# A fused attention and sparse feed forward kernel on one core: the feed forward's x and inner values are turned by VectorE and device memory instead of TensorE

## The reference

```python
def ffn(x, c1_w, c2_w, w1, w2t):            # x: [2048, 512]
    inter = x @ c1_w.T @ c2_w.T             # rank 16, then 1792 wide
    blk = inter.reshape(2048, 56, 32)
    idx = argmax(blk, axis=-1) + arange(0, 1792, 32)   # one of each 32
    h = relu(einsum('bkm,bm->bk', w1[idx], x))
    return einsum('bk,bkm->bm', h, w2t[idx])

x = x + tanh(g_xattn[0]) * xattn(layernorm(x), ctx, mask, bias, Wq, Wk, Wv, Wo)
x = x + tanh(g_ffn[0]) * ffn(layernorm(x), c1_w, c2_w, w1, w2t)
```

## Time and profile before

| | |
|---|---|
| median of 3 runs | 1841.38 us (1840.96 to 1842.55) |
| the profiled execution | 1842.1 us |
| its span, first to last instruction | 1840.3 us |
| TensorE busy | 1818.5 us, 13916 matmul records |
| VectorE, ScalarE, GpSimd busy | 1148.5, 683.3, 844.5 us |
| moved by DMA | 359.34 MB |
| projections, attention, feed forward | to about 930, to about 1475, to the end |

### The profile page before, as it was taken

One profiled execution on the slowest core, in us unless ns is written; L12 is line 12 of the kernel. 1 busy time (PEld: TensorE's weight loads), 2 busy tenths in 40 slices (PEclk: granted clock), 3 DMA queues, 4 the chain that ended last, 5 costly groups with the idle time before them and its releaser, 6 DMA issues.

```text
span 1840.3 us, 35211 instructions
## 1 busy us (share of the span) xinstructions
PE 1818.5 (99%) x13916; PEld 1509.9 (82%) x13916; DVE 1148.5 (62%) x1798; ACT 683.3 (37%) x1761; POOL 844.5 (46%) x734
## 2 busy tenths in 40 slices
PE   9999999999999999999999999999999999999999
PEld 7788878788888878888878888888888888888887
DVE  6566567544556673334357666786667887777773
ACT  5232324322333343233345555555555422222221
POOL 7734538755334887778734343343433121111110
PEclk9999999999999999999999999999999999999999
DMA  5554556444444644467658878798787650000000
GB/s 223 189 176 179 200 195 240 149 180 176 177 164 153 204 165 167 163 227 247 212 232 350 325 289 328 285 388 327 296 326 274 250 206 24 24 24 24 24 12 18
DMA packets 114900, 359.34 MB, mean 195 GB/s; under 512 B 12080, under 2 KB 20656, under 8 KB 104240
## 3 DMA queue, kind: packets, MB, share of 16 engines
q1 hardware_dynamic: 114736, 357.09, 52.7%
HBM read 229.11 MB, written 127.93 MB: 194 GB/s over the span
## 4 chain that ended last, share of the span: by engine, by line
PE 60%; DVE 2%; DMA 0%; ACT 0%; issue 0%; DVEq 0%; ACTq 0%
PE bank L1535 17%; PE bank L1537 16%; PE bank L1536 16%; PE bank L1640 4%; PE bank L1604 3%; PE bank L1620 2%; PE bank L1753 1%; PE bank L1730 1%; DMA x_tile<-in_x 0%; PE bank L1709 0%; ACT scores L940 0%; DVE attn_sum L1343 0%; DVE scores L1229 0%; DVE attn_t_lo L1315 0%; DVE scores L1217 0%
## 5 line engine op out<-in xcount | busy, mean ns | idle before, releaser
L1535 PE MATMUL bank<-tokens_hi,wkq_hi 128*128 128x512 f32 x888 | 346.7, 390 | 6.5 <-issue 4.0
L1536 PE MATMUL bank<-tokens_lo,wkq_hi 128*128 128x512 f32 x888 | 345.6, 389 | 0.0
L1537 PE MATMUL bank<-tokens_hi,wkq_lo 128*128 128x512 f32 x888 | 345.5, 389 | 0.0
L802 POOL TENSOR_TENSOR wkq_lo<-raw_wkq,wkq_hi 128x768 fp32r<-128x768 f32 x126 | 276.6, 2215 | 129.7 <-ACT wkq_hi L904 129.7
L1535 PE MATMUL bank<-wo_hi,attn_t_hi 128*128 128x512 f32 x512 | 205.7, 402 | 1.2 <-DVE attn_t_lo L1315 1.2
L1535 PEld LDWEIGHTS bank<-tokens_hi,wkq_hi 128*128 128x128 f32 x888 | 166.7, 188 | 44.7 <-issue 5.9
L1537 PE MATMUL bank<-wo_hi,attn_t_lo 128*128 128x512 f32 x512 | 199.8, 390 | 0.0
L1536 PE MATMUL bank<-wo_lo,attn_t_hi 128*128 128x512 f32 x512 | 199.3, 389 | 0.0
L1537 PEld LDWEIGHTS bank<-tokens_hi,wkq_lo 128*128 128x128 f32 x888 | 166.7, 188 | 34.7
L1536 PEld LDWEIGHTS bank<-tokens_lo,wkq_hi 128*128 128x128 f32 x888 | 166.7, 188 | 34.3
L940 ACT ACTIVATE scores<-scores,negmax 128x64 f32<-128x64 f32 x512 | 172.2, 337 | 41.8 <-DVE negmax L1222 41.8
(11 more groups left out here) (140 smaller groups left out, 3705.8 us busy)
## 6 DMA issues: line engine op xcount, KB each, us to landing
k_t<-c SPq DMA_DIRECT2D x128, 256.0 KB, 2.0
v_by_token<-c SPq DMA_DIRECT2D x128, 256.0 KB, 2.0
q_t<-c SPq DMA_DIRECT2D x128, 256.0 KB, 2.3
kt<-k_t SPq DMA_DIRECT2D x16, 2048.0 KB, 9.2
qt<-q_t SPq DMA_DIRECT2D x16, 2048.0 KB, 13.7
v<-v_by_token SPq DMA_DIRECT2D x16, 2048.0 KB, 12.6
raw_wkq<-in_wk SPq DMA_DIRECT2D x32, 512.0 KB, 4.3
raw_wv<-in_wv SPq DMA_DIRECT2D x16, 1024.0 KB, 8.3
```

The costliest lines, as they stand in the source:

```text
L802: pool.tensor_tensor(lo, job_raw(r)[:, a:b, :].rearrange("p a (c w) -> p a c w", c=2), hi.bitcast(F32), ALU.subtract)\
L1535: pe.matmul(o, a[0], b[0], start=first_mm, stop=False, skip_group_check=not grouped)
L1536: pe.matmul(o, a[0], b[1], start=False, stop=False, skip_group_check=not grouped)
L1537: return pe.matmul(o, a[1], b[0], start=False, stop=last_mm, skip_group_check=not grouped)
```

## The change

The transposes leave TensorE. The norm of an x tile is written to one buffer (`fxn`), VectorE turns it in 32 x 32 blocks (one instruction, into `fxb`), SyncE stores it to device memory (`xf_d`) and loads it back with an address pattern that puts the blocks in their places (`xfr`). ScalarE makes the high part from there, and GpSimd, no longer VectorE, the low part (`pool_fx` counts them). The inner values go the same way, in two halves of 1024 and 768 (`turn_h`, `store_h`, `load_h`, `HALF`), and GpSimd makes their low parts (`pool_hl`). Rows of c1, w1 and w2 are reordered on the host to suit. c1 is stacked so that one matmul with the high part of x and one with the low part do the low rank product: 8 in place of 12.

Hidden products now run two tiles ahead of the output, selectors three, and VectorE, ScalarE and GpSimd follow. x is prepared one tile in each iteration, in place of two in every second; six tiles (`X_EARLY`) are normed and turned during the attention. Nine x buffers replace five. Three of the seven loads of w2 are issued from ScalarE's queue. The lines of the core, cut:

```diff
-X2R = 5
+X2R = 9
+X_EARLY = 6
+HALF = [(0, 1024), (1024, 768)]
...
+    sel, hid = (2, 3), (4, 5, 1, 6, 0)
...
+            def store_h(t, i):
+                sp.wait_ge(dve_hb, 2 * t + i + 1)
+                sp.dma_start(h_d[i][t], hmb[i][:, :]).then_inc(h_out[i], 16)
+
+            def load_h(t, i):
+                sp.wait_ge(h_out[i], 16 * (t + 1))
+                if t:
+                    sp.wait_ge(pool_hl, 4 * (t - 1) + 2 * i + 2)
+                sp.dma_start(hraw[i][:, :, :], h_d[i][t].rearrange("(q g) (r f) -> (g r) q f", q=4, r=4))\
+                    .then_inc(h_in[i], 16)
...
+            def fx_lo(t):
+                pool.wait_ge(act_fx, t + 1)
+                pool.tensor_tensor(xft_part(t, 1), by_chunk(xfr[t % 2], 0, CH), xft_part(t, 0).bitcast(F32), ALU.subtract)\
+                    .then_inc(pool_fx, 1)
+
+            def ht_lo(t, g):
+                pool.wait_ge(act_h, 4 * t + g + 1)
+                pool.tensor_tensor(hmt_part(g, 1), hraw_part(g), hmt_part(g, 0).bitcast(F32), ALU.subtract)\
+                    .then_inc(pool_hl, 1)
...
-            for j in range(PAIRS):
-                if j % 2 and j + 4 < PAIRS:
-                    do_rstd(LN + j + 3)
-                    do_rstd(LN + j + 4)
-                if j + 2 < PAIRS:
-                    rank(j + 2)
+            for g in range(4):
+                ht_lo(0, g)
+            for j in range(-1, PAIRS):
+                if j > 0:
+                    for g in range(4):
+                        ht_lo(j, g)
+                if j + 7 < PAIRS:
+                    do_rstd(LN + j + 7)
+                if j + 3 < PAIRS:
+                    rank(j + 3)
+                if j + 5 < PAIRS:
+                    fx_lo(j + 5)
...
+            load_w2(5)
+            load_w2(6)
+            load_w2(4)
+            for j in range(-1, PAIRS):
+                if j >= 0:
+                    for g in range(4):
+                        ht_hi(j, g)
                 for k in range(4):
...
+                    if j + 3 < PAIRS:
+                        sel(j + 3, k)
+                if j + 5 < PAIRS:
+                    fx_hi(j + 5)
...
+            def turn_h(t, i):
+                a, w = HALF[i]
+                dve.wait_ge(dve_hm, 4 * t + 2 * i + 2)
+                if t:
+                    dve.wait_ge(h_out[i], 16 * t)
...
+                dve.transpose(hmb[i][:, :], hm[:, a:a + w]).then_inc(dve_hb, 1)
...
+            for j in range(-1, PAIRS + 1):
+                if j < 0:
                     low_rank(1)
...
+                if 0 <= j and j + 6 < PAIRS:
+                    f_norm((j + 6,))
+                if j + 2 < PAIRS:
+                    block_rank(j + 2)
+                if j % 2 and 0 < j and j + 3 < PAIRS:
+                    low_rank((j + 3) // 2)
+                if j + 2 < PAIRS:
+                    first_max(j + 2)
+                if j > 0:
                     finish(j - 1)
                 for k in range(4):
...
+                        pick_h(j + 2, k)
+                        if k % 2:
+                            turn_h(j + 2, k // 2)
+                    if j + 3 < PAIRS:
+                        block_max(j + 3, k)
+                    if k == 2 and j + 7 < PAIRS:
+                        f_stats((j + 7,))
+                if j + 3 < PAIRS:
+                    mark_max(j + 3)
...
             def low_rank(u):
                 pe.wait_ge(*bank_free(("t", u)))
-                pe.wait_ge(dve_fx, 2 * u + 2)
+                pe.wait_ge(pool_fx, 2 * u + 2)
...
+            for j in range(1, PAIRS + 1):
                 for k in range(4):
                     output(j - 1, k)
-                    transpose_h(j, k)
...
+                    if j == 1 and k < 2:
+                        selector(3, k + 2)
+                    if k == 1 and j % 2 and j + 3 < PAIRS:
+                        low_rank((j + 3) // 2)
                 for k in range(4):
+                    if j + 2 < PAIRS:
+                        hidden(j + 2, k)
+                    if j + 3 < PAIRS:
+                        selector(j + 3, k)
```

More of the change, by code:

```diff
@@ new lines, in next_of @@
+    def next_of(banks, use):
+        k = used.get(banks, 0)
+        used[banks] = k + 1
+        return (use, banks[k % len(banks)])
+    sel, hid = (2, 3), (4, 5, 1, 6, 0)
+    out = [(("t", 0), 0), (("sel", 0, 0), 7), (("sel", 0, 1), 0)]
+    out += [next_of(sel, ("sel", 0, k)) for k in (2, 3)]
+    out += [next_of(sel, ("sel", 1, k)) for k in (0, 1)]
+    out += [next_of(hid, ("h", 0, k)) for k in (0, 1)]
+    out += [next_of(sel, ("sel", 1, k)) for k in (2, 3)]
+    out += [next_of(hid, ("h", 0, k)) for k in (2, 3)]
@@ new lines, in ffn_uses @@
+    out.append(next_of(sel, ("t", 1)))
+    out += [next_of(hid, ("h", 1, 0)), (("h", 1, 1), 7), next_of(sel, ("sel", 2, 0))]
+    for k in (2, 3):
+        out += [next_of(hid, ("h", 1, k)), next_of(sel, ("sel", 2, k - 1))]
+    out += [next_of(hid, ("h", 2, 0)), next_of(sel, ("sel", 2, 3))]
+    out.append(next_of(hid, ("h", 2, 1)))
+    for k in (2, 3):
+        out += [next_of(hid, ("h", 2, k)), next_of(sel, ("sel", 3, k - 2))]
+    for j in range(1, PAIRS + 1):
+        out.append(next_of(hid, ("out", j - 1)) if j == PAIRS - 1 else (("out", j - 1), 7))
+        if j == 1:
+            out += [next_of(sel, ("sel", 3, k)) for k in (2, 3)]
+        if j % 2 and j + 3 < PAIRS:
+            out.append(next_of(sel, ("t", (j + 3) // 2)))
+        for k in range(4):
@@ L160, in ffn_uses @@
             if j + 2 < PAIRS:
-                out.append((("sel", j + 2, k), 2 + k % 2))
-    out.append((("out", PAIRS - 1), 7))
-    return [(use, (0, 7, 2, 3, 4, 5, 6, 1)[b]) for use, b in out]
+                out.append(next_of(hid, ("h", j + 2, k)))
+            if j + 3 < PAIRS:
+                out.append(next_of(sel, ("sel", j + 3, k)))
+    return out
 def build(nc, x, ctx_t, bias, mask, gates, wq, wk, wv, wo, c1, c2, w1, w2, out):
@@ L358, in build @@
         out_sem = [sem(f"dma_out{i}") for i in range(X2R)]
-        pe_x = sem("pe_ffn_xt")
+        xf_out = [sem(f"dma_ffn_xn_by_block{i}") for i in range(2)]
+        xf_in = [sem(f"dma_ffn_raw_xft{i}") for i in range(2)]
+        h_out = [sem(f"dma_h_by_block{i}") for i in range(2)]
+        h_in = [sem(f"dma_raw_h_t{i}") for i in range(2)]
         pe_t = sem("pe_ffn_t")
@@ L739, in _ @@
                         load_w1(n)
-                if s == SLOTS - 6:
-                    load_x2(3)
+                for t in range(X_EARLY):
+                    if s == SLOTS - 22 + 2 * t:
+                        load_x2(t)
+                    if s == SLOTS - 14 + 2 * t:
+                        store_xf(t)
+                    if t < 4 and s == SLOTS - 11 + t + t // 2 * 5:
+                        load_xf(t)
                 if it % G == G - 1 and it < ITERS:
@@ L1703, in _ @@
             scores(2)
[L1705 to L1711 removed]
             def low_rank(u):
                 pe.wait_ge(*bank_free(("t", u)))
[L1715 removed]
+                pe.wait_ge(pool_fx, 2 * u + 2)
                 if u == 0:
                     pe.wait_ge(*split_done(piece_no[("c1", 0)]))
[L1718 to L1720 removed]
+                for k, x_part in enumerate(xft[u % 2]):
+                    for c in range(CH):
+                        mm = pe.matmul(bank[f_bank[("t", u)]][:, 0:FU], c1s[:, c, :], x_part[:, c, :],
+                                       start=k == 0 and c == 0, stop=k == 1 and c == CH - 1)
                 mm.then_inc(pe_t, 1)
```

336 lines of the change are left out of this document (144 added, 192 removed).

## The result

The changed kernel takes **1864.58 us** (median of four runs, 1863.62 to 1865.89); the kernel before, 1841.51 beside it. The ratio is 1.0123, with a 95% interval of 1.0111 to 1.0135: 23.1 us slower, where 5.5 were forecast.

What follows compares the result with a forecast made beforehand. TensorE, busy 99%, was taken to bound the kernel. −37.1 us of gain, +20.3 for the first wait and +22.3 for steady waits gave +5.5: 1847 us, forecast case 1843 to 1853, range 1834 to 1860.

Steps and rivals of the forecast that it cites:

- The gain, 37.1 us: TensorE in the feed forward: 36.4 us less from removed transposes and low rank matmuls, plus a 0.7 us wait gone.
- The steady waits: TensorE at the low rank, iterations 3 to 11, waiting for GpSimd's low part of x: five waits, 22.3 us with collisions.
- T + 5.5 against T + 9.6: From output k=0's start T: TensorE reaches the low rank at T + 5.5, GpSimd's low part ends at T + 9.6.
- the norm ahead of the multiply: VectorE's norm shuts out GpSimd's rank multiply in each steady period: 0.5 us, making waits of 4.7.
- The first wait: TensorE at iteration 1's low rank, from 1511.2, because marks of tile 3 come late: 16.5 us, 20.3 with collisions.
- the added norms and turns in the attention: Layer norm and turn of six tiles on VectorE, about 2.1 us more per double slot, costed at nothing.
- The late data of tile 0: Rival: at 8 us a leg h tile 0's trip collides with w2 loads, delaying tile 2's multiply; no chance given.
- the collisions counted in this chain: First wait: VectorE's marks and norm and GpSimd's low parts and multiply block each other, 4.2 us in all.
- The clock: Rival: TensorE's clock falls to 1.2 GHz in the waits, 2 us for each of six, 1859 us; chance 0.13.
- No collision: Rival: VectorE and GpSimd do not shut each other out; sum −0.3 us, time 1841; chance 0.2.
- short waits: Rival: low parts of x ready by T + 5.5; 1825 without steady waits, 1804 without the first either; chance 0.2.
- That the change doesn't do what it says: Rival answered by the queues' order, which shows all 288 transposes gone; no chance given.

Runs made afterwards that it cites:

- Experiment 1: Changed kernel with GpSimd's low part of x tile j+5 ahead of the variance root and rank multiply of tile j+3: 1827.43 us.
- experiment 5: Kernel before the change with one transpose left of each feed forward group, most turned columns missing, for timing alone: 1828.46 us.
- experiment 4: Changed kernel with VectorE's norm and turn of x tile j+6 behind the block rank of tile j+2: 1864.53 us.
- experiment 11: Kernel of experiment 10 with norm and turn of x tile 5 moved behind VectorE's first low rank stack in the attention: 1816.80 us.
- experiment 3: Changed kernel with the last three pairs of w2 pieces loaded later, behind ScalarE's selector copies of tile 2: 1860.48 us.
- experiment 2: Changed kernel with 161 matmuls that nobody reads ahead of TensorE's six waits at the low rank: 1851.70 us.
- experiment 8: Changed kernel with TensorE's low rank behind the iteration's first hidden block instead of the second output group, GpSimd's order untouched: 1835.31 us.
- experiment 10: Changed kernel with x's low part first, early stack, later w2 loads and low rank of tiles 4 and 5, earlier tile 2 multiply and tile 0 finish: 1819.53 us.

## Why the prediction was wrong

- **The gain, 37.1 us:** right. Experiment 1's sum closes on it within 1 us, and in experiment 5 a single transpose of h costs the 0.11 us that the forecast took; what that kernel gained less was lost in new waits and late starts.
- **The steady waits:** right in place, cause and number. T + 5.5 against T + 9.6, with the norm 4.7 each; measured 4.19 and, in the last, 3.3, in all 20.0 for 22.3. The 0.5 for the norm ahead of the multiply was the part that was too large: 0.2 (experiment 4).
- **The first wait:** 22.9 for 20.3, and TensorE arrived at 1515.3, not at 1511.2, so its end was 6.7 us late. The terms that failed: for the added norms and turns in the attention, costed "at nothing; if the cover were gone, up to 1 us at the first selector", TensorE waited 1.41 us there, and the first hidden block started at 1474.65 instead of 1473.3 (experiment 11 takes 0.4 of the 1.41 away by moving one norm; that the rest is theirs isn't shown). The late data of tile 0, "2 to 3 us more", made the multiply of tile 2 end 10 us late; I had priced the trip, but not the single buffer into which the next tile is turned, and experiment 3 gives w2's share of it as 4.1 us of the time. TensorE's pauses at the end of that trip, 0.34 and 1.48 ahead of output 0, weren't in the sum. Of the collisions counted in this chain, 4.2 us, the one ahead of the multiply came (four low parts 6.25 us, for 3.5 x 1.27 = 4.4, beside the marks), the others made 0.7 us at most: from the multiply's end to the low part's end the chain took 19.6 us, and 18.9 in the forecast without them.
- **The clock: the step that failed.** It was the rival at 0.13, with "2 us for each of six waits 1859". All six waits had it, with 2.1 us on average: 12.4 by the trace, some 12 by experiment 2. Without it the time would have been 1852, inside the forecast's 1843 to 1853. The forecast rested on "the granted clock is 1.00 in every stretch, ... with waits of 2.4 us at most", which says nothing of waits of 4 and 20 us; as the forecast itself had six such waits in it, the slow clock belonged into its sum, and the range's upper edge of 1860 left out the dear half of it. The bound worked out there, up to 5.1 us a wait, holds. By it all six waits would have cost 31, by the rows 12. The Trainium skill, TensorE: Matmul & The Clock Gate, "Why this matters for your kernels", warns of exactly such gaps, and the trace agrees: 0.57 of full clock in 1586 to 1590.
- **Together:** of the 17.6 us between forecast and result 16.3 lie ahead of TensorE's end (forecast 1842.8; its last output matmul starts at 1858.63 and takes 0.4): 4.0 for the late arrival, 2.6 for the longer first wait, −2.3 for the steady waits, 12.4 for the clock, in all 16.7, which is 0.4 too much. The other 1.3 us are 0.4 behind TensorE's last matmul and 0.9 between the two profiled executions and the medians.
- **No collision, short waits:** the first sum has two slips (it takes 16.5 for 1527.3 − 1511.2 = 16.1, and 20.3 for 4 x 4.1 + 3.3 = 19.7, so that it is 1 us too high). It didn't decide anything, since the collision's price was small in the periods; the second is what experiment 1 makes by one move, 1827 us where the prediction had 1825 without the steady waits. That the two are so near is in part luck: its first wait is shorter, too (5.9 and 10.5 for 20.3), and the clock takes 3.1 of that back.
- **That the change doesn't do what it says:** it did.

What stays open: why a wait of 2.7 us is followed by the slow clock in one run and not in another, and so how much of experiment 11's 2.7 us is the moved norm's.

## What to carry to other kernels

When work is moved from the engine that bounds to one with time to spare, read the new queue in order: an instruction that the bound engine needs early (here 1.3 us of low part) must not stand behind one that waits for somebody's last instruction (here the multiply behind the marks). And price each wait that a forecast puts on TensorE twice, once for itself and once for the slow matmuls behind it: here 1.4 to 2.7 us, 2.1 on average, for each wait of 3.3 us or more. At the seam between two stages look at single buffers and at what else is in the DMA queues in those 20 us; averages over the steady loop say nothing about it.

## What the runs showed of the hardware

- A wait of 3.3 or 4.2 us is enough for the granted clock to fall, and it can do so only behind it: in the second wait it is still 1.00 in 1582 to 1586, and 0.57 in the four us behind, with TensorE busy. In the third it is 0.81 in the last four us of the wait. The waits of 1.07 us (the five later ones of experiment 8) and 1.41 us (at 1461) were not followed by it; those of 3.3 us and more all were. In between both happened: in experiment 10 a wait of 2.47 wasn't, and those of 2.53 (only 2.1 us of matmuls behind the 2.47) and 2.72 were; in experiment 11 one of 2.46 was and one of 2.72 wasn't; in experiment 2 the 2.47 left of the first wait wasn't.
- Matmuls that nobody reads, put in the waits, kept it at 1.00 and saved 12.9 us. As a mend it is second best: the same waits, taken away by order, gave 37.
- A *busy* instruction can be a waiting one. In experiment 1 VectorE is busy for 19.3 of 20 us in 1560 to 1580, which looks like a bound; its norms and first maxima from 1600 to 1700 (count, busy us, mean ns, idle time before them):

```profile
L1234 DVE TENSOR_SCALAR xn<-x_tile,ln_mean_var,ln_rstd 128x512 f32<-128x512 f32 x5 | 18.8, 3762 | 2.7 <-POOL ln_rstd L888 2.7
L1509 DVE TENSOR_TENSOR first_max<-is_max,block_first 128x1792 bf16<-128x1792 bf16 x5 | 12.7, 2537 | 0.2
```

A norm takes 0.54 us elsewhere and 3.76 here, as it starts while GpSimd multiplies; the first maxima take 2.54 instead of 2.02. A median beside a minimum shows it (539 and 3731 ns for the same shape), a busy share doesn't. The Trainium skill, SBUF — State Buffer, "Who interferes with whom", has a rule for VectorE in its two-port modes: whoever issues first blocks the other for its whole instruction. For the norm that comes second the trace agrees (3.71 and 3.76 us), though no run shows in which mode the norm works. For the multiply that comes second the rows don't decide: it loses 0.23 us to a norm with 0.38 us left. The norm has one tile and two columns of 128x1 for inputs; the prediction counted it among the instructions with two operands in SBUF, and no run here tells which of its inputs matters.
